# A graph-network stack: the steps of the load, and the residual add of the first layer, rearranged

## What is computed

```
h = relu(layernorm(x)); x = x + leaky_relu(D(adj + I)D @ concat(h[:2048] @ Wr, h[2048:] @ Wd) + bias, 0.01)
h = relu(layernorm(x)); x = x + two GraphSAGE convolutions: relu(concat(h, adj @ h) @ W1), then the same with W2
h = relu(layernorm(x)); x = x + relu(D(adj + I)D @ h @ W.T + b)
h = relu(layernorm(x)); x = x + elu(concat(att @ h, -att_negative @ h) @ wtrans), masked softmax attention
```

## Time and profile before

| what | value |
|---|---|
| time, median of 3 runs | 2162.99 us (2162.39 to 2164.28) |
| time of the profiled execution | 2162.58 us |
| span in that profile | 2160.8 us |
| TensorE busy | 2066.9 us (96%) |
| VectorE busy | 1411.4 us (65%) |
| ScalarE busy | 1442.5 us (67%) |
| GpSimd busy | 2.2 us |
| mean DMA rate over the span | 134 GB/s |

### The profile page before, as it was taken

The page is one execution under the profiler, slowest core; times in us unless marked ns, Lnnn a source line. Parts: engine busy times, 40 slices in busy tenths (PEclk is TensorE's granted clock), DMA queues, the critical chain, the costliest instruction groups (busy, mean ns, idle before and its releaser), DMA issues.

```text
span 2160.8 us, 26784 instructions
## 1 busy us (share of the span) xinstructions
PE 2066.9 (96%) x10560; PEld 1500.1 (69%) x10560; DVE 1411.4 (65%) x2220; ACT 1442.5 (67%) x1762; POOL 2.2 (0%) x12
## 2 busy tenths in 40 slices
PE   4788899999989999999999999999999999999998
PEld 3677776555555555545455478888888888888887
DVE  5778586000024243324456989999999999999664
ACT  5665577555546554566665578788887878787963
POOL 0000000000000000000000000000000000000000
PEclk9999999999999999999999999999999999999999
DMA  9898335101130222311119664445444536352300
GB/s 319 306 320 302 115 118 199 45 20 39 36 120 11 78 65 53 127 66 59 59 35 277 193 225 148 168 139 185 148 175 142 195 116 221 103 215 71 109 20 10
DMA packets 102687, 289.35 MB, mean 134 GB/s; under 512 B 45217, under 2 KB 52129, under 8 KB 86049
## 3 DMA queue, kind: packets, MB, share of 16 engines
q1 hardware_dynamic: 96320, 276.10, 37.8%
q10 hardware_dynamic: 6240, 11.54, 1.6%
HBM read 245.63 MB, written 33.58 MB: 129 GB/s over the span
## 4 chain that ended last, share of the span: by engine, by line
PE 86%; DVE 6%; ACT 4%; DMA 2%; issue 2%; SPq 0%; POOL 0%; DVEq 0%; ACTq 0%; POOLq 0%
PE ps L1733 40%; PE ps L1644 31%; PE ps L1661 6%; PE ps L1529 4%; PE ps L1703 2%; ACT work L605 2%; PE ps L1587 1%; ACT big L605 1%; PE ps L1575 1%; PE ps L1613 1%; DMA feat<-in_adj 1%; DMA feat<-in_adj_t 1%; DMA work<-in_adj_t 1%; DVE work L1256 0%; DVE stat L1284 0%
## 5 line engine op out<-in xcount | busy, mean ns | idle before, releaser
L1644 PE MATMUL ps<-work,feat 128*128 128x512 bf16 x3072 | 668.8, 380 | 4.8 <-DVE feat L1210 4.3
L605 ACT ACTIVATE work<-big 128x1024 bf16<-128x1024 uint8 x440 | 459.9, 1053 | 315.5 <-PE ps L1644 306.2
L1644 PEld LDWEIGHTS ps<-work,feat 128*128 128x128 f16 x3072 | 300.9, 98 | 366.5 <-issue 6.8
L1733 PE MATMUL ps<-big 128*128 128x257 f32 x2048 | 451.9, 381 | 3.3 <-ACT big L934 3.3
L1733 PE MATMUL ps<-big,work 128*128 128x257 f32 x2048 | 450.9, 381 | 4.1 <-ACT work L934 4.0
L1733 PEld LDWEIGHTS ps<-big 128*128 128x128 f32 x2048 | 390.4, 191 | 59.7 <-ACT big L934 3.7
L1733 PEld LDWEIGHTS ps<-big,work 128*128 128x128 f32 x2048 | 388.4, 190 | 60.1 <-issue 4.8
L1529 PE MATMUL ps<-feat,work 128*128 128x256 f16 x2048 | 230.4, 274 | 25.0 <-ACT work L605 17.6
L1529 PEld LDWEIGHTS ps<-feat,work 128*128 128x128 bf16 x2048 | 199.8, 98 | 54.0 <-ACT work L605 19.7
L926 ACT ACTIVATE big<-feat,uv_sb 128x512 f32<-128x512 f32 x256 | 163.3, 710 | 20.2 <-PE ps L1733 20.2
L926 ACT ACTIVATE work<-feat,uv_sb 128x512 f32<-128x512 f32 x256 | 163.4, 713 | 15.4 <-PE ps L1733 14.2
(11 more groups left out here) (159 smaller groups left out, 1367.5 us busy)
## 6 DMA issues: line engine op xcount, KB each, us to landing
big<-in_adj_t SPq DMA_DIRECT2D x64, 1024.0 KB, 4.9
feat<-in_adj SPq DMA_DIRECT2D x56, 1024.0 KB, 7.0
work<-in_adj_t SPq DMA_DIRECT2D x86, 512.0 KB, 6.3
feat<-in_adj_t SPq DMA_DIRECT2D x42, 512.0 KB, 6.3
h_spill<-work SPq DMA_DIRECT2D x32, 512.0 KB, 3.6
feat<-h_spill SPq DMA_DIRECT2D x32, 512.0 KB, 4.8
x_spill<-work SPq DMA_DIRECT2D x24, 512.0 KB, 2.7
work<-x_spill SPq DMA_DIRECT2D x16, 512.0 KB, 3.9
```

The lines of the kernel that those rows point to most:

```text
L605: return nc.scalar.activation(out_, in_, ACT.Copy, **kw)
L1644: ins = mm(ps[:, bank + f, :], parts[:, j, h, f * P:(f + 1) * P], stage[:, g % STAGES, jj, :], start=(fresh and h == 0), stop=(end and h = ...
L1733: ins = mm(ps[:, 4 * s + t, 0:YW], quads[k % RING][:, jj, t * P:(t + 1) * P], Yb[:, j, s, :], start=(j == 0), stop=(j == NT - 1), skip_gro ...
```

## The change

The tiles of `h` start earlier in the load and closer together (`H0_AT`, one chunk in five steps and not in six or seven), all 32 tiles alternate between two PSUM banks, and VectorE copies the products of chunks 4 and 5 too (`Y0_DVE` 6). Statistics are taken two tiles to a step, two steps later against the tiles. SyncE's first loads are reordered. `save_sums(5)` moves from step 7 to step 0 of chunk 7 in ScalarE's program. In layer 0 GpSimd adds the residual (`residual`) between ScalarE's leaky ReLU and VectorE's statistics, and two of ScalarE's seven stagings move in between the leaky ReLUs of tiles 1, 2 and 3.

```diff
@@ -51,8 +51,8 @@
     EVACS = [0, 1, 1, 1]
     KB = [4, 4, 4, 2]
     SLOT = [0, 2, 6, 0, 2, 6, 4, 2]
-    H0_AT = [4, 10, 17, 23, 30, 36, 43, 49]
-    Y0_DVE = 4
+    H0_AT = [0, 5, 10, 15, 20, 25, 30, 35]
+    Y0_DVE = 6
     RESTARTED = {2: 0, 3: 1, 4: 2, 5: 3, 7: 5}
     EARLY = 7
     Y_BANKS = 4
@@ -177,11 +177,11 @@
         def h0_t(n):
 
             k = n % 2
-            return ps[:, 4 if k == 0 and n < 6 * TPC else 6, k * 2 * P:(k + 1) * 2 * P].rearrange("p (k n) -> p k n", k=FB)
+            return ps[:, 4 + 2 * k, k * 2 * P:(k + 1) * 2 * P].rearrange("p (k n) -> p k n", k=FB)
 
         def y0_ps(n):
 
-            return ps[:, 5 if n % 2 == 0 and n < 6 * TPC else 7, 0:F]
+            return ps[:, 5 + 2 * (n % 2), 0:F]
 
         def y0_at(c, t):
 
@@ -219,6 +219,7 @@
         scaled_ready, hi_split, split_done = sem("scaled_ready"), sem("hi_split"), sem("split_done")
         panel_ready, group_done = sem("panel_ready"), sem("group_done")
         own_in, own_added = sem("own_in"), sem("own_added")
+        residual_added = sem("residual_added")
         evac_done, out_ready = sem("evac_done"), sem("out_ready")
         out_used = [sem(f"out_used{l}") for l in range(4)]
         hs_ready, hi_ready, post_done = sem("hs_ready"), sem("hi_ready"), sem("post_done")
@@ -370,10 +371,12 @@
 
 
             load_x(x_in, 0, 0)
+            for g in range(2):
+                load_piece(0, g)
             sp.dma_start(w_sb[:, 0:KB[0], :], w_gcn.rearrange("(k p) f -> p k f", p=P)).then_inc(weights_in, 16)
-            for g in range(NQ):
+            load_x(x_in, 1, 1)
+            for g in range(2, NQ):
                 load_piece(0, g)
-            load_x(x_in, 1, 1)
 
             def pieces(c, first=0):
                 for g in range(first, GROUPS):
@@ -589,9 +592,24 @@
                 nc.gpsimd.affine_select(out=eye[:, :], in_=eye[:, :], compare_op=ALU.not_equal, fill=1.0, base=0,
                                         pattern=[[-1, P]], channel_multiplier=1).then_inc(consts_ready, 1)
 
-            for n in range(2):
+            def largest(n):
+
                 pool.wait_ge(gown_ready, n + 1)
                 nc.gpsimd.partition_all_reduce(g_all, g_own, P, bass.bass_isa.ReduceOp.max).then_inc(gall_ready, 1)
+
+            def residual(c, t):
+
+                if t == 0:
+                    pool.wait_ge(x_in_s[c % 2], c // 2 * 16 + 16 * (X_USES[0] * H + 1))
+                pool.wait_ge(out_used[0], c * TPC + t + 1)
+                x_t = x_ring[:, c % 2, t, :]
+                nc.gpsimd.tensor_tensor(x_t, hs32[:, t % 2, :], x_t, ALU.add).then_inc(residual_added, 1)
+
+            largest(0)
+            for c in range(NC):
+                for t in range(TPC):
+                    residual(c, t)
+            largest(1)
 
 
             pool.wait_ge(panel_ready, staged(4))
@@ -689,12 +707,12 @@
                     if c == 0 and g == GROUPS - 1:
                         act.wait_ge(wa_ps_ready, 1)
                         copy(wa_sb[:, :, :], ps[:, 3, 0:2 * FB].rearrange("p (k s) -> p k s", s=2)).then_inc(wa_ready, 1)
-                    if c > 3 and g == (7 if c == 7 else 0):
+                    if c > 3 and g == 0:
                         save_sums(c - 2)
 
-            def leaky(c):
-
-                for t in range(TPC):
+            def leaky(c, tiles):
+
+                for t in tiles:
                     act.wait_ge(linear_ready, c * TPC + t + 1)
                     nc.scalar.activation(hs32[:, t % 2, :], hs32[:, t % 2, :], ACT.Prelu, alpha=SLOPE)\
                       .then_inc(out_used[0], 1)
@@ -812,7 +830,11 @@
 
                     for c, m in enumerate((10, 17, 24, 31, 38, 45, 52, 59)):
                         done = stage_next(m)
-                        leaky(c)
+                        leaky(c, (0, 1))
+                        done = stage_next(m + 1)
+                        leaky(c, (2,))
+                        done = stage_next(m + 2)
+                        leaky(c, (3,))
                         done = stage_next(m + 3)
                         post_std(c)
                         done = stage_next(m + 4)
@@ -1171,9 +1193,9 @@
                             y0_low(c - 1, g - 4)
                     for e, first in enumerate(H0_AT):
                         for t in range(TPC):
-                            if n == max(first - 5 + t, 0):
+                            if n == max(first - 3 + t // 2, 0):
                                 x_stats(e, t)
-                        if n == first - 1:
+                        if n == max(first - 1, 0):
                             means(e)
                     if c > 0:
                         for m, pair in staged_at(c, g):
@@ -1276,10 +1298,13 @@
                                                            ALU.mult, ALU.add).then_inc(out_used[l], 1)
                         if t > 0:
                             mean_and_variance(t - 1, ch.link)
-                        dve.wait_ge(out_used[l], i0 + (t + 1))
+                        if l == 0:
+                            dve.wait_ge(residual_added, i0 + t + 1)
+                        else:
+                            dve.wait_ge(out_used[l], i0 + (t + 1))
                         if l == 3:
                             ch.link(nc.vector.scalar_tensor_tensor(x_t, y_t, 0.0, x_t, ALU.max, ALU.add))
-                        else:
+                        elif l == 2:
                             ch.link(nc.vector.tensor_tensor(x_t, y_t, x_t, ALU.add))
                         ch.link(nc.vector.bn_stats(stat[:, t, :], x_t))
                     last_variance(ch.link)
@@ -1570,7 +1595,7 @@
 
             def h0_transposed(n):
                 pe.wait_ge(h0_done, n + 1)
-                wait(pe, h0_t_evac, n - 1 if n < 6 * TPC else n)
+                wait(pe, h0_t_evac, n - 1)
                 for k in range(FB):
                     ins = mm(h0_t(n)[:, k, :], hs32[:, n % 2, k * P:(k + 1) * P], ident32[:, :], start=True, stop=True,
                              skip_group_check=True)
@@ -1581,7 +1606,7 @@
                 if n == 0:
                     pe.wait_ge(weights_in, 16)
                 pe.wait_ge(h0_t_evac, n + 1)
-                wait(pe, y0_out, n - 1 if n < 6 * TPC else n)
+                wait(pe, y0_out, n - 1)
                 wait(pe, var_ready, summed)
                 for k in range(FB):
                     ins = mm(y0_ps(n), T32[:, n % 2, k, :], w_sb[:, FB * (c // H) + k, :], start=(k == 0), stop=(k == FB - 1),
```

## The result

The changed kernel takes 2138.14 us (median; 2136.79 to 2141.46), beside 2162.69 us for the kernel before. The ratio is 0.9889, with a 95% interval of 0.9872 to 0.9907: 24.5 us or 1.1% less. Forecast were 2147 us and at the least 2139. The direction was right, and so were the three places; each of the three gains was larger than forecast. In the changed kernel the lines have other numbers: L605 is L623 (L606 is GpSimd's add), L1529 is L1554, L1567 L1592, L1083 L1105, L1256 L1278, L1284 L1309, L1030 L1052, L1644 L1669.

A forecast was written before the change was run, and what follows sets the result against it. TensorE was busy 2066.9 of 2160.8 us, so only 94 us of idle time, mostly in the load, could be gained. -3 - 8 - 5.5 = -16.5 us from 2162.99 gave 2146.5, said as 2147 us, range 2139 to 2157.

The forecast's parts named there:

- Part 1: Load: tiles of h move (steps, banks, copies, first loads); -3 us, from -9 to +4.
- The late x: Load: x is asked for four steps ahead, before five, so VectorE may wait; 0.5 us charged in all.
- Part 2: Chunk 7 of the load: `save_sums(5)` at step 0 brings chunk 7 from 36 to 28 us; -8, from -3 to -9.5.
- The gap: Chunk 7: TensorE's 9.51 us gap after the degree sums, ended by ScalarE's `save_sums(5)` copy; 8 us to be gained.
- Part 3: Rest of layer 0 after the load: GpSimd's add and ScalarE's order; -5.5 us, from -8 to 0.
- The pace: Rest of layer 0: VectorE's `post` per chunk with a saved part falls from 14.26 to 13.0 us, without one to 12.1.
- The round trip: Rest of layer 0: GpSimd's add plus handover in each tile's chain, taken as 0.75 + 0.1 = 0.85 us.
- the two engines hinder each other: Rest of layer 0: GpSimd's adds and VectorE's scalings delay each other, up to 1.9 us a chunk; 2152 us, chance 0.13.
- the crowded start isn't given back: Load: chunks 0 and 1 cost 7.5 us, chunk 2 gains only 4, x comes late; 2154 us, chance 0.12.
- the ring as the bound of chunk 7: Chunk 7: the four-slot ring sets the pace, 33 us, so -3 in place of -8; 2152 us, chance 0.09.
- The slower rival: Rest of layer 0: the add's round trip becomes the bound; 2175 us, chance 0.05 shared with late x at every chunk.

The follow-up runs named there:

- The order alone: Kernel before with only ScalarE's new order, two stagings moved in between the leaky ReLUs, VectorE still adding: 2157.19 us beside 2162.05.
- The add alone: Kernel before with only the residual add moved to GpSimd, ScalarE keeping its old order: 2162.05 us beside 2164.03, ratio 0.9991.
- the doubled add: Changed kernel with a second GpSimd add of the same size into scratch ahead of each real one: 2154.84 us, ratio 0.9958.

## Why the prediction was wrong, point by point

**Where the time was to come from: right.** The load and the rest held it, everything in front of layer 1 went through to the end (24.0 us there, 24.5 in the medians), and the three parts add up. The marks that the prediction named came out so: chunk 2 far under 30 us, no gap over 2 us before chunk 7's first pair, part chunks every 13.1 us, layer 1 at 331.65 and not near 339.

**Part 1, forecast -3, measured -6.4 by the degree sums and -7.4 alone.** The mechanism was right: chunks 0 and 1 pay, chunk 2 gives back. The medians leave it uncertain by 3 us, and the means over the traces are 5.6 us apart; by each of these it is more than was forecast. The terms that were mis-sized: I charged VectorE's added work in full (+4 and +3.5) where +3.4 and +2.5 came, and took 10 us for chunk 2, where 8.9 came. The largest miss is chunk 3: I gave it only 1 us, holding 24 us for the pace of the transfers because chunk 4 took that; it ran in 23.0 us from 26.3, at 395 GB/s, so chunk 4's 370 GB/s were no bound. The 36 and 25 us of the windows were cut to whole numbers; the marks say 35.3 and 26.3. The late x did show, once: VectorE waited 1.2 us for `in_x`. The two banks, which I put among the reasons for chunk 2, are worth about 1 us of it. Two sums of its range are off as well: with no charge in chunks 0 and 1 it is -10.5 and not -9, and with a gain of 4 us in chunk 2 it is +3 and not +4.

**Part 2, forecast -8, measured -9.9 and -9.0 alone.** The gap went as described, with its 1.58 us left. What I sized wrong is the line "I count nothing for it beyond the 28 us": the lower clock behind the stop was 2.2 us of matmul time. The two lengths were windows' too: chunk 7 was 37.1 us long by the marks, not 36, and chunks 5 and 6, from which I took the 28 us, are 27.0 each; it took 27.3. I also wrote that TensorE was busy 24 of 25 us in chunks 3 and 4 at a clock of 1.00; the earlier trace rows have that for chunk 3 and 20.9 of 24 us for chunk 4.

**Part 3, forecast -5.5, measured -7.8 and -7.7 alone.** Here the step itself failed: "of the idle time there stay 4 x (13.0 - 12.4) = 2.4 us". The pace came out right (13.1 us, and 12.1 to 12.2 without a part where I had 12.1), with some luck: the last statistics of a part chunk come 0.76 us earlier and not 1.05, and what I had added for jitter made up for it. The round trip came out near (0.97 us from the end of the leaky ReLU to the statistics, where I had 0.85). But a pace above TensorE's 12.4 us only costs when the staged lead is used up. At 13.1 us the product is 2.8 us, and none of it is there: behind the rest's first pairs TensorE never waits. The order alone shows the lead: at a pace of 13.86 us the same product is 5.8 us, and 2.8 are paid, where the kernel before pays 7.0 of 7.4. So the order gives 2.5 us of lead, which I had at nothing. The gains in pace don't stand by themselves either, as I had them. The add alone changes the pace by 0.26 us, the order alone by 0.40, both by 1.16: the add's 0.76 us reach the root only when the order has made ScalarE free for it.

**The rivals.** That the two engines hinder each other didn't carry this kernel (0.1 us a chunk), but as a mechanism it is real: with the doubled add a scaling takes 0.74 us in place of 0.48. That the crowded start isn't given back is refuted, as is the ring as the bound of chunk 7. The slower rival was right as a mechanism, as the doubled add shows, and its price didn't arise: the round trip is 0.97 to 1.05 us, against the 1.55 us from which a part chunk would lose.

The three errors had one sign, and together they are 7.6 us. The low end of 2139 us is 24 us under the kernel before. The low ends given for the three parts (-9, -9.5, -8) add up to 26.5 us, or 2136.5, so it left out the case that all three come out large, which is what happened.

## What to carry to other kernels

Where a bound engine is fed through a few staged slots by another that also serves a slower chain, move the stagings in between that chain's waits before shortening the chain: the order gave 4.9 us where the shortened chain alone gave 2, and half of the 4.9 was lead, which a sum of pace against pace doesn't have. When work is taken off one arm of a join, look what the other arm does at that moment; if it has just entered a group of long instructions, they are the new wait. And cost a stop of TensorE with the slower matmuls behind it.

## What the runs showed of the hardware

GpSimd's float32 add of two 128x256 tiles took 0.72 to 0.73 us, VectorE's 0.425; from the end of the leaky ReLU to its start and from its end to the statistics it was 0.14 and 0.12 us. That is a ratio of 1.7; the Trainium skill ("GPSIMD Engine Reference", section 3.1) has 1.96 for tiles of 2048 columns. Behind a stop of TensorE of 9.5 us the granted clock was 0.50 for 3 us and 0.78 for 4 more, and 224 matmuls took 26.95 us in place of 24.8. Of a GpSimd add and a VectorE scaling with two SBUF tiles, the one that started second took longer: the scaling 0.74 to 0.75 us in place of 0.48, the add 0.82 to 0.92 in place of 0.72.
